# An attention kernel whose last unit is summed at once: new order table, new start order, nine probability slots for ten

## The reference

```
xn  = layernorm(x)
q   = xn Wq (16 heads of 64);  latent = xn Wkv_down (64);  k = latent Wk_up;  v = latent Wv_up
att = softmax(causal(q k^T / 8));  a = (att v) Wout
f   = tanh(xn W W1 W2 + bias)
out = x + a + f
```

## Time and profile before

| | |
|---|---|
| runs | 1958.07 us, median of 3 (1958.02 to 1961.17) |
| profiled execution, own time | 1955.77 us |
| its span | 1954.1 us |
| TensorE (PE) | busy 1930.8 us, 99% of the span |
| GpSimd (POOL) | 1456.2 us, 75% |
| VectorE (DVE) | 1366.3 us, 70% |
| ScalarE (ACT) | 1143.7 us, 59% |
| granted TensorE clock, mean | 0.999 of 2.4 GHz |

### The profile page before, as it was taken

One profiled execution on the slowest core, in us unless ns is written; L12 is line 12 of the kernel. 1 busy time (PEld: TensorE's weight loads), 2 busy tenths in 40 slices (PEclk: granted clock), 3 DMA queues, 4 the chain that ended last, 5 costly groups with the idle time before them and its releaser, 6 DMA issues.

```text
span 1954.1 us, 38790 instructions
## 1 busy us (share of the span) xinstructions
PE 1930.8 (99%) x13536; PEld 1310.7 (67%) x13536; DVE 1366.3 (70%) x3626; ACT 1143.7 (59%) x2201; POOL 1456.2 (75%) x1277
## 2 busy tenths in 40 slices
PE   8999999999999999999999999999999999999998
PEld 7667666667666666666666667666666666666664
DVE  7778666787578766698666967658567795666662
ACT  5565655656565655665556556556565565665562
POOL 1778678777787877887677887787777867788782
PEclk9999999999999999999999999999999999999999
DMA  5122121321222121231112212122121221222110
GB/s 144 46 72 61 53 56 47 83 56 53 53 62 76 50 56 53 59 85 53 45 48 71 73 48 61 53 69 64 47 67 45 83 58 37 61 61 58 42 45 28
DMA packets 117599, 116.50 MB, mean 60 GB/s; under 512 B 24092, under 2 KB 100764, under 8 KB 117404
## 3 DMA queue, kind: packets, MB, share of 16 engines
q1 hardware_dynamic: 117404, 114.02, 21.5%
HBM read 53.67 MB, written 8.91 MB: 32 GB/s over the span
## 4 chain that ended last, share of the span: by engine, by line
PE 92%; DVE 6%; issue 1%; ACT 1%; DMA 1%; POOL 0%; SPq 0%; ACTq 0%; DVEq 0%; POOLq 0%
PE ps L1074 25%; PE ps L999 21%; PE ps L1092 14%; PE ps L1056 13%; PE ps L1059 13%; PE ps L1119 3%; DVE split_lo L1369 1%; DVE ps L1329 1%; PE ps L1105 1%; DVE maxima L1334 1%; PE ps L1151 1%; DMA probs<-in_L_attn_Wq 0%; PE ps L1032 0%; DVE x_in L1434 0%; PE ps L1173 0%
## 5 line engine op out<-in xcount | busy, mean ns | idle before, releaser
L1494 POOL TENSOR_TENSOR p_sum<-p_sum,probs 128x512 f32<-128x512 f32 x660 | 850.6, 1319 | 133.7 <-ACT probs L1229 132.7
L1229 ACT ACTIVATE probs<-ps 128x512 f32<-128x512 f32 x1152 | 660.5, 597 | 300.4 <-PE ps L1059 282.3
L1329 DVE CUSTOM_DVE_ANT_0 ps<-ps,causal 128x512 f32<-128x512 f32 (+4 forms) x1024 | 521.3, 527 | 229.2 <-PE ps L1092 221.3
L1074 PE MATMUL ps<-probs,latent 128*32 128x512 f32 x4608 | 518.1, 594 | 0.3 <-DVE q_lo L1457 0.3
L1092 PE MATMUL ps<-k_hilo,q_hi 128*128 128x512 f32 (+4 forms) x1536 | 481.7, 356 | 5.9 <-DVE maxima L1329 1.9
L1056 PE MATMUL ps<-q_hi,k_hilo 128*128 128x512 f32 x1152 | 467.8, 406 | 1.8 <-ACT probs L1229 0.8
L1059 PE MATMUL ps<-q_lo,k_ones 65*128 65x512 f32 x1152 | 457.1, 397 | 0.0
L1334 DVE TENSOR_REDUCE maxima<-ps 128x1 f32<-128x512 f32 (+1 forms) x512 | 326.0, 637 | 152.8 <-PE ps L1092 148.2
L1494 POOL TENSOR_TENSOR p_sum<-probs 128x512 f32<-128x512 f32 x222 | 288.3, 1314 | 164.0 <-ACT probs L1229 159.1
L1074 PEld LDWEIGHTS ps<-probs,latent 128*32 128x32 f32 x4608 | 139.0, 110 | 316.3 <-issue 312.3
L1092 PEld LDWEIGHTS ps<-k_hilo,q_hi 128*128 128x128 f32 x1536 | 281.4, 189 | 100.0 <-issue 21.9
(11 more groups left out here) (110 smaller groups left out, 2258.8 us busy)
## 6 DMA issues: line engine op xcount, KB each, us to landing
q_hi<-q_hi SPq DMA_DIRECT2D x256, 128.0 KB, 2.4
norm<-recips SPq DMA_DIRECT2D x254, 128.0 KB, 2.9
q_lo<-q_lo SPq DMA_DIRECT2D x128, 128.0 KB, 2.4
x_in<-in_L_attn_x_bld SPq DMA_DIRECT2D x16, 512.0 KB, 4.6
acc<-in_L_attn_x_bld SPq DMA_DIRECT2D x32, 256.0 KB, 2.9
out_x<-acc SPq DMA_DIRECT2D x64, 128.0 KB, 1.7
q_lo<-rows SPq DMA_DIRECT2D x128, 4.0 KB
rows<-norm SPq DMA_DIRECT2D x127, 4.0 KB
```

The source lines that it names most:

```text
L1074: last = nc.tensor.matmul(y_bank[row:row + WIDTH, :], latent[par][:, key_block(unit, s), half:half + WIDTH], probs[:, t % PT_SLOTS, g * BA ...
L1229: nc.scalar.activation(probs[:, t % PT_SLOTS, g * BANK:(g + 1) * BANK], ps[:, bank_of[kind, key], :], ACT.Exp).then_inc(exp_done, 1)
L1329: nc.vector.tensor_tensor_reduce(bank, bank, causal[:, BANK - w:BANK], 1.0, LOWEST, ALU.add, ALU.max, maxima[:, unit % 4, h, 0:1]).then_in ...
L1494: nc.gpsimd.tensor_tensor(sums, other, probs[:, slot, part], ALU.add).then_inc(pool_done, 1)
```

## The change

1. **The last unit.** GpSimd adds its steps into `p_sum` like any other's, all but the last step. `R` of unit 127 then makes the broadcast sum at once: four products on `p_sum` and four on the last step's probabilities. The multiplication (`DM`, new) follows each half's reciprocal and reads the result of `PV` from PSUM; it was copied out by ScalarE and read from there. 
2. **Where the late halves lie.** For units 124 to 127 the high and low halves are written into query buffers that are no longer used (`split_of`), so that `HI` and `HF` need not wait for the output product of the unit before.
3. **Slots.** `PT_SLOTS` 10 to 9, `SUM_SLOTS` 2 to 3.
4. **The start.** Wq is loaded in two halves, the first ahead of Wk; the conversion of Wkv ("casts") moves from VectorE to GpSimd; the first fold of wqk comes before the transposes of x; a key product of the first half of tokens needs only that half's transposes; the queries of half 1 are made among the foldings; other banks are used.
5. **The order table.** `SEGMENT` 36 to 24 and 24 rows of `RULES` for 16, all of them new, and the times that the planner starts from are other ones. The plan of the whole body is laid anew.

The diff, cut to its core:

```diff
-PT_SLOTS, Y_SLOTS, SPLIT_SLOTS, SUM_SLOTS, Q_BUFS = 10, 3, 1, 2, 3
+PT_SLOTS, Y_SLOTS, SPLIT_SLOTS, SUM_SLOTS, Q_BUFS = 9, 3, 1, 3, 3
-SEGMENT = 36
+SEGMENT = 24
 RULES = [
-    (7, 11, 0, 1.5, 300, 600, 0),
...
+    (10, 12, 0, 1.0, 300, 2000, 800),
...
@@ first_plan
-    plan += [("LN4", (0, k)) for k in range(2)] + [("W", "turn wk"), ("W", "turn wq")]
-    plan += [("T", (0, c, 0)) for c in range(2)] + [("LN4", (0, k)) for k in range(2, 4)]
-    plan += [("TL", (0, c, 0)) for c in range(2)] + [("W", "casts"), ("W", "fold wqk 0")]
-    plan += [("T", (0, c, 1)) for c in range(2)] + [("TL", (0, c, 1)) for c in range(2)]
+    plan += [("LN4", (0, k)) for k in range(4)]
+    plan += [("W", "turn wq 0"), ("W", "turn wk"), ("W", "turn wq 1"), ("W", "fold wqk 0")]
+    for side in range(2):
+        plan += [("T", (0, c, side)) for c in range(2)] + [("TL", (0, c, side)) for c in range(2)]
...
-    plan += [("W", "fold aux"), *maxima[2:5], ("W", "fold wvo"), *maxima[5:], ("W", "fold wff")]
-    plan += [("MT", 0), ("W", "split wvo"), *two_parts("Q", (1, 0)), *two_parts("Q", (1, 1))]
-    plan += [("QL", (1, 0)), ("QD", (1, 0)), ("XA", 0), ("XA", 1), ("XA", 2)]
-    plan += [("QL", (1, 1)), ("QD", (1, 1))]
+    plan += [("W", "fold aux"), *maxima[2:5], *two_parts("Q", (1, 0)), ("W", "fold wvo")]
+    plan += [*maxima[5:], *two_parts("Q", (1, 1)), ("QL", (1, 0)), ("MT", 0), ("W", "fold wff")]
+    plan += [("QL", (1, 1)), ("W", "split wvo"), ("QD", (1, 0)), ("QD", (1, 1))]
+    plan += [("XA", 0), ("XA", 1), ("XA", 2)]
@@ load_all
+                (wq_in[:, :, 0:4 * P], wq_rows[:, :, 0:4 * P], wq_loaded[0]),
                 (wk_in, Wk_up.rearrange("c h k -> c (h k)"), wk_loaded),
-                (wq_in, Wq.rearrange("(c p) h k -> p c (h k)", p=P), wq_loaded),
+                (wq_in[:, :, 4 * P:8 * P], wq_rows[:, :, 4 * P:8 * P], wq_loaded[1]),
@@ make_constants (GpSimd)
+            pool.wait_ge(wkv_loaded, 16)
+            for cols in both:
+                nc.gpsimd.tensor_copy(wkv_hi[:, :, cols], wkv_in).then_inc(consts_made, 1)
+            pool.wait_ge(consts_made, 10)
+            for cols in both:
+                nc.gpsimd.tensor_tensor(wkv_lo[:, :, cols], wkv_in, wkv_hi[:, :, cols].bitcast(F32),
+                                        ALU.subtract).then_inc(consts_made, 1)
@@
+        def split_of(unit, final):
+            if unit >= final - 3:
+                n = 2 * (final - unit) % 4
+                free = (q_hi if unit >= final - 1 else q_lo)[(final // 2 - 2) % Q_BUFS]
+                free = free[:, :, :].rearrange("p (n j) q -> p n (j q)", n=4)
+                return free[:, n, :], free[:, n + 1, :]
+            return split_hi[:, unit % SPLIT_SLOTS, :], split_lo[:, unit % SPLIT_SLOTS, :]
@@ TensorE, after each PV
-                    if unit == final and s < block_of(unit):
-                        if s == 0:
-                            take_bank("R", unit)
-                        broadcast_sums(t, s == 0, False)
@@ TensorE, R of the last unit
-                    broadcast_sums(first_step(key) + block_of(key), False, True).then_inc(p1_full, 1)
+                    bank, last_step = take_bank(kind, key), first_step(key) + block_of(key)
+                    wait_new(pool_done, 2 * last_step)
+                    broadcast_sums(bank, lambda part: p_sum[:, key % SUM_SLOTS, part], True, False)
+                    wait_new(exp_done, 2 * last_step + 2)
+                    broadcast_sums(bank, lambda part: probs[:, last_step % PT_SLOTS, part], False,
+                                   True).then_inc(p1_full, 1)
@@ ScalarE, HF
                     act.wait_ge(last_divided, 2 * part + 2)
-                    if part == 0:
-                        act.wait_ge(p1_full, count.p1("O", unit - SPLIT_SLOTS) + 1)
@@ VectorE, DM
+                elif kind == "DM":
+                    unit, part = key
                     dve.wait_ge(last_divided, 2 * part + 1)
-                    nc.vector.tensor_tensor(y[:, slot, cols], y[:, slot, cols], norm[:, slot, cols],
+                    nc.vector.tensor_tensor(y[:, slot, cols], norm[:, slot, cols],
+                                            ps[:, bank_of["Y", unit], cols],
                                             ALU.mult).then_inc(last_divided, 1)
@@ GpSimd
-                if unit == final:
+                if unit == final and s == block_of(unit):
                     continue
```

More of the change, by code:

```diff
@@ L260, in flush @@
                 self.multiplied[key] = self.run("POOL", when, (1300, 1350))
-                if key < SPLIT_SLOTS or key - SPLIT_SLOTS in self.out:
+                if key == 0 or (key - SPLIT_SLOTS in self.out if key < self.units - 4
+                                else key - 1 in self.halved):
                     self.after(self.multiplied[key], "HI", key)
             elif kind == "HI":
+                self.halved.add(key)
+                if key >= self.units - 5 and key + 1 in self.multiplied:
+                    self.after(max(when, self.multiplied[key + 1]), "HI", key + 1)
                 self.after(self.run("ACT", when, ACT_TIME[kind]), "LO", key)
@@ L285, in choices @@
                     out.append((max(q + LATER["Q"], self.earliest("MAX")), self.max_at[self.n_max] - lead, self.place_max))
+        if self.sums and self.sums[0][1] == self.units - 1:
+            out.append((max(self.masked[-4:]), now - 9, self.place_r))
         if "P1" in self.open:
@@ L384, in place_p1_half @@
         self.out[u] = done
-        for part in range(2):
-            if (u + 1, part) in self.multiplied:
-                self.after(max(done, self.multiplied[u + 1, part]) + part, "HF", (u + 1, part))
-        if u + SPLIT_SLOTS in self.multiplied:
+        if u + SPLIT_SLOTS in self.multiplied and u + SPLIT_SLOTS < self.units - 4:
             self.after(max(done, self.multiplied[u + SPLIT_SLOTS]), "HI", u + SPLIT_SLOTS)
@@ L407, in place_r @@
         if u == self.units - 1:
-            done = self.on_pe("R", ready, PE_TIME["PV"])
+            self.takes("MAX", "R", u)
+            done = self.on_pe("R", ready, (1720, 1930))
             for part in range(2):
-                self.after(max(done, self.y_copied[u]) + part, "DV", (u, part))
+                self.after(done + 2 * part, "DV", (u, part))
+                if self.n_pv == len(self.steps):
+                    self.after(done + 2 * part + 1, "DM", (u, part))
             return
@@ L471, in place_pvs @@
                 self.takes("Y", "Y", u)
+            final = u == self.units - 1 and s == block_of(u)
             self.plan.append(("PV", (t, u, s)))
@@ L474, in place_pvs @@
             self.pv.append(end)
-            if u == self.units - 1 and s < block_of(u):
-                if s == 0:
-                    self.takes("MAX", "R", u)
-                self.free["PE"] += PE_TIME["PV"][0]
+            if final:
+                if u in self.summed:
+                    for part in range(2):
+                        self.after(end + part, "DM", (u, part))
             elif s == block_of(u):
@@ L482, in place_pvs @@
         self.n_pv += n
-        while self.sum_ready() <= self.free["PE"] + self.soon:
+        while self.sums and self.sums[0][1] < self.units - 1 and self.sum_ready() <= self.free["PE"] + self.soon:
             self.place_r(self.sum_ready())
@@ L489, in sum_ready @@
         at, u = self.sums[0]
-        if u == self.units - 1 and self.n_pv < len(self.steps):
-            return 1e12
         return max(at, self.earliest("P1")) if u < Y_SLOTS or u - Y_SLOTS in self.normal else 1e12
@@ L512, in build @@
                     continue
-                if self.sum_ready() < 1e12:
+                if self.sum_ready() < 1e12 and self.sums[0][1] < self.units - 1:
                     self.place_r(self.sum_ready())
@@ L552, in body_plan @@
     return plan, order.bank
-FIRST_Q = (4, 3)
 def first_plan():
```

171 lines of the change are left out of this document (92 added, 79 removed).

## The result

| | before | changed |
|---|---|---|
| runs | 1958.05 us, median of 4 (1956.78 to 1961.17) | 1983.18 us, median of 4 (1978.32 to 1993.13) |
| ratio | | 1.0135, 95% interval 1.0112 to 1.0158 |
| profiled execution, own time | 1955.77 | 1987.03 |
| its span | 1954.1 | 1985.3 |
| granted clock, mean | 0.999 | 0.990 |

The changed kernel is 25 us slower. The forecast was 1950.5, with a range that ended at 1957 and a chance of 0.08 for slower: wrong in sign, and outside the range.

What follows compares the result with a forecast made beforehand. TensorE's own work in series was taken as the bound. Start -0.5, body 0, end -3.0 and -3.6, clock +0.6 gave -6.5; with -1.0 more in the body, -7.5 us: median 1950.5, range 1941 to 1957.

Steps and rivals of the forecast that it cites:

- The start: Up to the first scores: earlier folds and keys, a later row of maxima, less idle after; -0.5 us, between -2 and +1.5.
- The end, second part: Chain behind the last broadcast sum: reciprocal to last addition in 6.7 us for 11.1; with 0.8 ahead, -3.6 us.
- 0.6 for the clock: Last output product: PE idle some 3.3 us before it may run at 1.2 GHz; half of 1.2 us counted, +0.6.
- The end, first part: Ahead of the last broadcast sum: six of eight broadcast products go, but GpSimd has twelve more additions; -3.0 us.
- +0.8: Behind GpSimd's last sum: unit 126's subtraction stands ahead of the reciprocals, some 2.6 us against 1.8 for the broadcast sum.
- a tie: Stretch before the last broadcast sum: GpSimd 33.7 us against PE 34.0; with subtractions in the way, 0.7 us of waiting.
- The body: Windows from 44 to 1904 us: same items, only waits can change; 0, between -9 and +6 us.
- The sign that I had named for being wrong: The body's windows give or take more than 8 us by themselves.
- The slower rival: Throughout the body: VectorE's subtractions starved by GpSimd, four to five more such stalls; 1962 to 1966 us, chance 0.08.
- The -1.0 for the spare slot of sums: Body: half of the one large PE idle (2.48 us) goes, as a late sum has a spare slot; -1.0 us.

Runs made afterwards that it cites:

- ends_frozen: The changed kernel's new start and end, with the body's order and slots of the kernel before: 1951.53 us, ratio 0.9968.
- ends_gap_lo: `ends_frozen` with six GpSimd instructions around each late half waiting for the end of the one before: 1948.14 us, ratio 0.9939.
- before_gap_lo: The kernel before with six GpSimd instructions around each late half waiting for the end of the one before: 1956.21 us, ratio 0.9988.
- after_gap4: The changed kernel with 40 GpSimd instructions, around the late halves of units 79, 96, 98 and 123, waiting for the one before: 1950.45 us, ratio 0.9953.
- after_gap1: The changed kernel with 10 GpSimd instructions, around the late half of unit 79, waiting for the one before: 1965.63 us, ratio 1.0042.

## Why the prediction was wrong

**The start: right, in `ends_frozen` better than said.** Forecast -0.5 us. In `ends_frozen`, which has the body's order of before, the first row sum (`R` of unit 0) shows it, before and after:

```profile
63.45 0.64 PE L1119 MATMUL ps<-p_sum,ones 128*32 128x256 f32 x8
...
62.47 0.64 PE L1147 MATMUL ps<-p_sum,ones 128*32 128x256 f32 x8
```

-0.98. The first key product came at 17.25 in the changed kernel where I said 18.7; the first scores at 41.27 where I said 41.4, with 2.20 us of idle time ahead where I said 1.4. The row of maxima was what PE waited for, as forecast:

```profile
41.27 0.50 PE L1084 MATMUL ps<-q_hi,k_hilo 128*128 128x512 f32 x1 [2.20 <-DMA q_lo<-rows]
```

The idle time of 1.51 us just behind it is gone, as forecast. Not counted was the clock: in this trace products took 0.63 us for 0.40 around 44 us (0.98 over the window from 44), which gives back some 1.7 us by the estimate of half; `ends_frozen` has none of that.

**The end, second part: right.** From the first reciprocal to the last addition before took 11.1 us; the forecast was 6.7, and 0.6 for the clock. The chain of `ends_frozen`:

```profile
1939.37 1.77 DVE norm L1378
...
1944.19 2.41 PE ps L1025 x12
...
1946.63 0.42 DVE acc L1417
```

7.3 us, with the last products at the lower clock as feared (2.41 us). They took 1.67 in the changed kernel and 1.68 in `ends_gap_lo`, and the stretch 6.5 us in both: the low clock came in one of three.

**The end, first part: right in sign, too large.** Forecast -3.0 and +0.8, so -2.2 us at the first reciprocal. `ends_frozen` has it at the same time as before (1939.37 and 1939.42) while `R` of unit 125 was 0.6 us late (1913.57 for 1912.99): -0.6. The chain shows where the rest went: unit 124's subtraction took 1.74 us, PE stood idle for 1.00 before its product, and the twelve products behind it ran at a low clock, 2.51 us for 1.42.

```profile
1925.39 1.74 DVE q_lo L1407
...
1927.27 2.51 PE ps L1025 x12
```

With the gap around the late halves (`ends_gap_lo` against `before_gap_lo`) the same stretch gains 1.2 us. There the +0.8 came as said, the first reciprocal 0.8 us behind the broadcast sum; what was too small was PE's waiting ahead of the sum, 0.94 us for the exponential, 0.45 for unit 124's late half and 1.14 for GpSimd's sum:

```profile
1933.71 1.07 PE L1059 MATMUL ps<-p_sum,ones 128*32 128x512 f32 x8 [1.14 <-POOL p_sum L1549]
```

I had called it a tie with 0.7 us of waiting. Start and end together: forecast -6.5 (all but the body's -1.0), measured -5.4 (`ends_frozen`), -7.2 (with the gap everywhere) and -8.1 (with the gap around the late halves). **These terms held**, in their sum better than one by one: the start won more than said and the first part of the end less.

**The body: the step that failed.** "Body: 0, between -9 and +6". Without shut-outs the new order is equal to the old (+1.2 us with the gap around the late halves, -4.0 with the gap everywhere), so the zero was right for everything that I had weighed in it. The bound was not: against `ends_frozen` the body cost some 32 us. The bound came from the idle time that the trace of before had: 8.5 us in all, "a poor one can lose as much". But the kernel before held more risk than loss: seven subtractions of 3 to 9 us, 40.6 us in all, six of them hidden. The bound should have been what they cost uncovered: by the new trace, a wait costs PE its length less the some 3 us of work that PE has without VectorE, and 2 to 3 us behind it at half clock, so 8 to 9 us for a wait of 9.3. Four places of 11.8, 9.9, 7.3 and 6.2 us did cost some 36 in that execution. The sign that I had named for being wrong, more than 8 us given by the body's windows alone, is what came: 34.2 us of idle time for 8.7.

**The slower rival named the mechanism and mispriced it.** It said "One such subtraction cost PE 2.48 us", "four to five such stalls more than the one in the trace" and "Against it: of 127 only one did this". The first two took the cost of the one covered case for the price. The single place of unit 79 was worth about 11, so four places did it by far. The third counted stalls of PE, not shut-outs, of which there were seven. Rows 8 gave the most (9316 ns) and the median; asking for the distribution between, and for PE's work beside each, was the step left out.

The Trainium skill says of this port pair ("SBUF — State Buffer", section "SBUF: two separate sides") that whichever engine starts first has it for the whole instruction, and the other fully blocks. I had read that as one instruction of waiting. The trace agrees in the normal case: the median subtraction takes 1.00 us, 0.68 alone. It does not for the seven; the measurement decides, and the longest was passed over ten times.

**The -1.0 for the spare slot of sums** can't be judged. In `ends_frozen` (two slots, the order of before) that idle time stayed at 2.5 us behind the same 9.32 us; the new order has no such place, and no run has three slots with the order of before. Slots and table were not tried apart, since each changes what the planner makes of the other.

## What to carry to other kernels

- Where two engines share a port, look at every long instruction of the loser and at what the bound engine had to do beside it, not at the idle time that resulted. A hidden wait is a price that a new order can call in: its bound is the length of the winner's backlog, less the covered work, plus what the half clock takes behind it.
- When a reordering moves the time by more than its items explain, read windows for the few that are not full before looking for something spread out.
- One trace is a sample where an engine can be passed over: two of the places differed between executions of the same instructions. Compare a trace's sum with its own execution, not with the median.
- A wait that leaves a gap between the winner's instructions around the place where the loser comes (here 40, or some six in ten per unit) is a cheap mend; the gap everywhere costs 9 us in the kernel before.

## What the runs showed of the hardware

- A VectorE subtraction with two inputs in SBUF was passed over at up to ten instruction boundaries of GpSimd, additions, multiplications and masks alike, as long as each GpSimd instruction was queued behind the last; once GpSimd had nothing, it was done within 0.55 us. In all seven of the changed kernel over 2 us it ended 0.55 us after GpSimd's last instruction. With a wait for the former's end ahead of each mask and addition, none of 127 took over 1.8 us, in three kernels.
- A small instruction was held up too: a multiplication of 128x8 elements, both inputs in SBUF, took 4.34 us for a median of 0.63, and ended with the last GpSimd instruction that was queued.
- For one order it recurs: `ends_frozen` has 9.32, 7.50, 6.29 and 6.08 us where the kernel before has 9.32, 7.50, 6.32 and 6.07. It still varies between executions: unit 76 took 0.72 us in the changed kernel and 9.96 and 9.98 in two kernels that are the same up to there. What decides whether the first boundary is lost stays open.
- Behind PE's idle times of 3.2 to 9.6 us in the body its products ran at 0.50 of 2.4 GHz for a while, and a group of twelve took up to 2.93 us for 1.43. Behind an idle time of 2.4 us at one and the same place the clock fell in one execution (0.53, `after_gap4`) and not in another (1.00, `after_gap1`).
